# Weight splitting of the routed experts moved behind the last batch's gating in the shared-expert stage

## The reference

```
x2 = rmsnorm(hid, ln2_w)
logits = x2 @ gate_w.T
probs = softmax(logits);  top_w, top_i = top_k(probs, 4);  top_w /= top_w.sum()
routed = sum over the 4 chosen experts of top_w * (silu(g) * u) @ w2,   g, u = x2 @ w1
shared = (silu(sg) * su) @ sh_down_w.T,                                 sg, su = x2 @ sh_gu_w.T
out = hid + routed + shared
```

## Time and profile before

| | |
|---|---|
| median of 3 runs | 1240.77 us (1239.87 to 1243.07) |
| the profiled execution | 1242.91 us, with a span of 1241.2 us |
| PE busy, share of the span | 95% |
| DVE / ACT / POOL busy | 69% / 64% / 47% |
| mean granted clock of PE | 0.986 |
| shared-expert stage | 945.7 to 1012 us |
| tile loop | 1012 to 1199 us |

### The profile page before, as it was taken

One profiled execution on the slowest core, in us unless ns is written; L12 is line 12 of the kernel. 1 busy time (PEld: TensorE's weight loads), 2 busy tenths in 40 slices (PEclk: granted clock), 3 DMA queues, 4 the chain that ended last, 5 costly groups with the idle time before them and its releaser, 6 DMA issues.

```text
span 1241.2 us, 25176 instructions
## 1 busy us (share of the span) xinstructions
PE 1178.2 (95%) x7996; PEld 1007.7 (81%) x7996; DVE 861.5 (69%) x2662; ACT 794.0 (64%) x1971; POOL 577.1 (47%) x845
## 2 busy tenths in 40 slices
PE   6899999889999999999999999999998889999986
PEld 5756555579999998999989999989997769999962
DVE  5677887677667666886667876777865855555535
ACT  3387777767768776677676777776776534444422
POOL 3053645545333444537443366433363346666650
PEclk9989999999999999999999999999999989999998
DMA  8955555175733112122212122121214247777766
GB/s 266 283 160 174 172 167 152 51 213 152 213 109 95 54 55 87 48 70 83 86 35 69 35 68 105 35 68 35 69 61 113 68 124 122 117 118 119 117 113 218
DMA packets 111780, 139.59 MB, mean 112 GB/s; under 512 B 11364, under 2 KB 94820, under 8 KB 111524
## 3 DMA queue, kind: packets, MB, share of 16 engines
q1 hardware_dynamic: 97204, 119.10, 31.6%
q0 software_dynamic: 14448, 18.88, 9.4%
HBM read 63.36 MB, written 61.87 MB: 101 GB/s over the span
## 4 chain that ended last, share of the span: by engine, by line
PE 70%; DVE 12%; ACT 8%; issue 4%; POOL 3%; DMA 2%; SPq 1%; POOLq 0%; ACTq 0%; DVEq 0%
PE bank L1478 49%; PE bank L1887 5%; PE bank L1710 5%; DVE bank L1113 3%; PE bank L1527 3%; PE bank L1581 2%; ACT p L953 2%; PE bank L1564 2%; DVE hs L1336 2%; ACT pT L832 2%; DVE pT L1323 1%; PE bank L1866 1%; PE bank L1897 1%; PE bank L1571 1%; DVE qk L1212 1%
## 5 line engine op out<-in xcount | busy, mean ns | idle before, releaser
L1113 DVE CUSTOM_DVE_ANT_0 bank<-bank,mask 128x512 f32<-128x512 f32 (+3 forms) x512 | 235.2, 523 | 35.8 <-PE bank L1564 23.1
L944 ACT ACTIVATE p<-bank,stat 128x512 f32<-128x512 f32 (+3 forms) x256 | 131.7, 528 | 132.2 <-DVE stat L1113 132.2
L533 POOL CAST w_hl<-raw_qkv 128x512 fp32r<-128x512 f32 x96 | 58.8, 613 | 312.3 <-DMA raw_qkv<-in_qkvo 162.6
L1478 PE MATMUL bank<-xT,w_hl 128*128 128x512 f32 x768 | 189.2, 395 | 0.0
L1478 PEld LDWEIGHTS bank<-xT,w_hl 128*128 128x128 f32 x768 | 144.1, 188 | 34.1
L742 POOL DMA_INDIRECT sum_rows<-mid,goal x79 | 122.9, 1555 | 70.7 <-DVE mid L1442 69.2
L1478 PE MATMUL bank<-pT,v 128*128 128x128 f32 (+3 forms) x768 | 137.1, 327 | 0.0
L953 ACT ACTIVATE p<-p,stat 128x512 f32<-128x512 f32 (+3 forms) x256 | 123.1, 553 | 14.7 <-DVE stat L1339 14.7
L1478 PE MATMUL bank<-qk 128*128 128x512 f32 (+3 forms) x768 | 129.4, 317 | 3.2 <-DVE pT L1323 2.4
L1478 PEld LDWEIGHTS bank<-qk 128*128 128x128 f32 x768 | 119.3, 189 | 12.1 <-DVE v L1212 2.6
L534 POOL TENSOR_TENSOR w_hl<-raw_qkv,w_hl 128x512 fp32r<-128x512 f32 x96 | 124.2, 1294 | 7.8
(11 more groups left out here) (232 smaller groups left out, 2404.0 us busy)
## 6 DMA issues: line engine op xcount, KB each, us to landing
raw_qkv<-in_qkvo SPq DMA_DIRECT2D x32, 768.0 KB, 5.7
xs_rows<-blank SPq DMA_DIRECT2D x32, 520.0 KB, 3.3
xs_rows<-blank SPq DMA_DIRECT2D x5, 2730.0 KB, 14.3
xrow<-xs_rows SPq DMA_DIRECT2D x79, 130.0 KB, 2.5
raw_o<-in_qkvo SPq DMA_DIRECT2D x32, 256.0 KB, 3.7
sum_rows<-blank SPq DMA_DIRECT2D x3, 2176.0 KB, 8.5
stk<-xT SPq DMA_DIRECT2D x96, 64.0 KB
stk<-k_hl SPq DMA_DIRECT2D x96, 64.0 KB
```

What stands on the lines that cost most here:

```text
L944: act.activation(p2[:, n % 2, POFF[qi]:POFF[qi + 1]], s2(t), ACT.Exp, scale=-1.0, bias=stat2[:, 0, n % 2, t:t + 1], accum_out=stat2[:, 1, ...
L1113: return dve.tensor_tensor_reduce(scores, scores, mask[:, TB - scores.shape[1]:], scale=-1.0, scalar=-2.0 * MASKED, op0=ALU.add, op1=ALU.m ...
L1478: ins = pe.matmul(out, a, b, start=start and i == 0, stop=stop and i == len(pairs) - 1, **kw)
```

## The change

Four edits, none of which adds or removes an instruction.

1. ACT's four `w1_half` move from s = 0, 1, 6, 7 to s = 4, 6, 7, 8; DVE's four `w1_rest` from s = 1, 2, 10, 11 to s = 6, 7, 8, 10.
2. On DVE the sums of a finished batch (s = 3, 6, 9, 12) stand behind `hh_lo` and behind `probabilities` and `compare`, not ahead of them.
3. On PE the logits of the last batch stand ahead of `shared_down(1)`, not behind it.
4. PE's transpose of the tile table and DVE's copy into `tab` move from s = 7 to s = 8.

```
+        W1_STEPS, W1_REST_STEPS = (4, 6, 7, 8), (6, 7, 8, 10)
...
                 if s == 0:
-                    w1_half(0, 0)
                     norm_half(B - 1)
                 if s == 1:
                     for c in range(C):
                         take_x2(B - 1, c, bank[4 + c])
-                    w1_half(0, 1)
-                if s in (6, 7):
-                    w1_half(1, s - 6)
+                if s in W1_STEPS:
+                    w1_half(*divmod(W1_STEPS.index(s), 2))
                 if s in (5, 6, 7, 8):
                     fill_row(B - 1, s - 5)
...
                     dve.tensor_tensor(half, half, bank[2 + s % 2][0:rows, :], ALU.mult).then_inc(f_h, 1)
-                if s and s % SHR == 0:
-                    b = s // SHR - 1
-                    dve.wait_ge(f_dn, s)
-                    dve.wait_ge(r_row, TPB * (b + 1))
-                    for i in range(2):
-                        two = hs[:, TPB * b + 2 * i:TPB * b + 2 * i + 2, :].rearrange("p j d -> p (j d)")
-                        dve.tensor_tensor(two, two, bank[6 + i][:, :], ALU.add).then_inc(f_acc, 1)
                 if LO_POOL <= s < SHARED:
...
                 if s == 3:
                     probabilities(B - 1)
                     compare(range(0, 6))
+                if s and s % SHR == 0:
+                    b = s // SHR - 1
+                    dve.wait_ge(f_dn, s)
+                    dve.wait_ge(r_row, TPB * (b + 1))
+                    for i in range(2):
+                        two = hs[:, TPB * b + 2 * i:TPB * b + 2 * i + 2, :].rearrange("p j d -> p (j d)")
+                        dve.tensor_tensor(two, two, bank[6 + i][:, :], ALU.add).then_inc(f_acc, 1)
...
-                if s == 7:
+                if s == 8:
                     dve.wait_ge(r_tabT, 1)
                     dve.tensor_copy(tab[0:1, :], bank[4][0:1, 0:2 * P]).then_inc(r_tabi, 1)
-                if s >= SHARED - 2 and s < SHARED:
-                    w1_rest(1, s - SHARED + 2)
+                if s in W1_REST_STEPS:
+                    w1_rest(*divmod(W1_REST_STEPS.index(s), 2))
...
+                if s == 2:
+                    logits(B - 1, bank[4])
                 if s:
                     shared_down(s - 1)
...
-                if s == 2:
-                    logits(B - 1, bank[4])
...
-                if s == 7:
+                if s == 8:
                     pe.wait_ge(r_tab, 1)
```

More of the change, by code:

```diff
@@ L1401, in _ @@
                         take_x2(B - 1, c, bank[4 + c])
-                    w1_rest(0, 0)
                 if s == 2:
                     logits_less_max(B - 1, bank[4])
-                    w1_rest(0, 1)
                 if s == 3:
```

## The result

The changed kernel takes **1250.18 us** in the median of 5 runs (1248.46 to 1251.36), the kernel before 1243.07 in the median of its 5 runs (1239.87 to 1245.05): a ratio of 1.0059 with a 95% interval of 1.0043 to 1.0075, which is 5.3 to 9.3 us slower. The forecast was 1247.9, or +7.1; the difference of the medians is 7.1. The forecast counted from a median of three runs, 1240.77; with two more it is 1243.07, so the same step ends 2.3 us above the forecast time.

A forecast was written before the change was run, and what follows sets the result against it. The last send's landing was taken to set PE's loop start. Holds of 9.6 us, less the old hold 1.8 and the lead 0.7, gave +7.1 us: 1240.77 to 1247.9 us, forecast's own range 1244 to 1252.

The forecast's parts named there:

- What bounds it: Tile loop on PE: always busy, so a shift of its start, set by the last send's landing, shifts the end equally.
- The lead: Gating on DVE: wk written 0.7 us earlier, bounds 0.4 and 1.4, after POOL's hh_lo costs 0.7 to 1.0.
- The sends and `w_lo`: POOL's sends beside DVE: each of four w_lo holds one send until it ends, 9.6 us in all, 1.8 before.
- The phase: Sends against w_lo: a send beginning just before each w_lo makes every hold 1.8 and the sum +4.7 us.
- the prediction's last sentence: Sends beginning a little before each w_lo rather than after: every hold the small one, 1.8, sum +4.7 us.
- ACT's longer queue: ACT filling the third and fourth tiles, at 997.5 and 1002.5: hidden by the sends' own delay, ahead of their copies.
- The table's copy: DVE's copy into tab, a step later at 999.9: costs nothing, since SP waits for landings until 1016.
- PE's clock: PE at the loop's start: half-rate stretch (clock 0.66) taken as equal, with 1.5 us either way.
- the second rival: PE idles, then stays at half rate over steps 8 to 11: +12 to +14 us, 1253.5; chance 0.07.
- Rival 1: Sends not held by w_lo; third tile waits for ACT's xrow: +2.6 us, 1243.4, within 0.3%; chance 0.15.

The follow-up runs named there:

- e3: Changed kernel with the weight splitting back at its old steps (ACT 0, 1, 6, 7; DVE 1, 2, 10, 11), other three edits kept; 1242.89 us, ratio to before 1.0006.
- e5: Kernel before with the first edit alone (weight splitting at its new steps; sums, logits and table as before); 1247.40 us, ratio to before 1.0046.
- e1: Changed kernel with each w_lo's second operand from a PSUM bank, leaving out the subtraction of w_hi; 1241.49 us, ratio to before 0.9988.
- e11: Kernel before with the second operand of its last two w_lo from PSUM, leaving out that subtraction of w_hi; 1238.29 us, ratio to before 0.9976.
- e2: Changed kernel with each w_lo cut into four pieces, one behind the other; 1246.99 us, ratio to before 1.0035.
- e4: Changed kernel with ACT's fill_row ahead of w1_half in steps 6, 7 and 8; 1248.69 us, ratio to before 1.0053.
- e8: Changed kernel with each w_lo in four pieces and ACT's fill_row ahead of w1_half; 1247.28 us, ratio to before 1.0039.
- e9: Changed kernel with each w_lo in four pieces and the copy into tab behind the pieces of step 8; 1247.52 us, ratio to before 1.0045.

## Why the prediction was right, point by point

- **What bounds it.** Right: the loop's start carried over whole, 7.65 us there and 7.66 at the tail.
- **The lead** of 0.7 us in `wk` was 0.55. POOL's `hh_lo` beside the comparisons took its part: `compare`'s first instruction took 1.30 us in the changed kernel. But the lead hangs on the first edit alone: e3, without it, has `wk` 0.6 us late, and e5, with nothing else, has it 1.12 early. The working's parts came out: the probabilities at 967.25 (965.42 + 1.84), and the product of step 4 at 971.56, where 970.8 and the 0.7 to 1.0 of POOL's share give 971.5 to 971.8. What it did not ask is which edit gains. Against e5 the probabilities begin 1.8 us earlier (13.74, there 15.55), but the sums' 1.2 us follow before the product of step 4 all the same, and the earlier comparisons meet POOL's `hh_lo`: the other three edits together lose 0.57.
- **The sends and `w_lo`.** The step that carried the sum, from one send of 2.76 us. It is shown: with one operand in PSUM the hold is gone in both kernels (e1, e11), with shorter instructions it is shorter (e2), and it is in the first edit alone (e5). The four held sends and their order were as worked out; their holds were 9.6 by the working (2.0, 2.4, 2.5, 2.7) and 10.15 in the trace (1.84, 2.50, 2.91, 2.90). The whole was +7.1 by the working and +7.65 at the first tile. That the medians also differ by 7.1 to the tenth is luck, with an interval of 5.3 to 9.3. The phase was a near thing: two of the sends came 0.10 and 0.12 us behind the start of a `w_lo`. In e4 the fourteenth begins 0.38 us ahead of it, and the hold there is the small one, 1.79, as the prediction's last sentence has it. In e5 three of the four `w_lo` hold a copy, a case that the working left out.
- **ACT's longer queue** was hidden by the holds, as said: in e4 the first tile comes 0.45 us earlier and the ratio is 0.0006 lower, well inside both intervals. Its price without them is in e1: the last send begins 3.3 us later than in the kernel before, without holds.
- **The table's copy** a step later cost nothing: written at 998.6, while the last send landed at 1014.95.
- **PE's clock.** PE stood still for 1.84 us ahead of 984.70, 2.30 ahead of 993.00 and 1.81 ahead of 1005.18. The five-microsecond windows from 985 to 1015 have the clocks 0.66, 0.80, 0.86, 1.00, 0.66 and 1.00: half rate for a time after each, but not to the end of the stage; the second rival did not come. The prediction took the half-rate stretch at the loop's start as equal. It was (0.69 and 0.63 in the two five-microsecond windows from 1015, before 0.67 and 0.65 in the two from 1010), and e1 shows that it need not be.
- **Rival 1** is what e1 is: +2.6 us was said for no holds. At the first tile it was +3.2, at the tail +1.6, and in the median -1.0. Its mechanism held (the tile waits for `xrow`); its price left out that PE, hardly idle ahead of the loop, had clock 1.00 there. What makes the median lower still is not known.
## What to carry to other kernels

Where VectorE and GpSimd work side by side, list the VectorE instructions with two operands in SBUF and their lengths: here each held one GpSimd instruction that began inside it, an indirect DMA, a copy or a `tensor_tensor`, until it ended. Moving such an instruction off one chain is only a gain if GpSimd has nothing on the critical path where it lands; one send in a trace that is 2.9 times as long as its 63 fellows is reason enough to look at what VectorE did then. And look at what else moves when an order is changed for another reason: in e3 earlier logits put a VectorE instruction 0.1 us ahead of a GpSimd one, and the lead was gone; and sums that were moved back made TensorE wait for them.

## What the hardware showed that I had not expected

- An instruction of DVE that begins 0.1 us ahead of POOL's `hh_lo` made it 4.17 us in place of 1.29 (e3); in the other order, DVE's 0.08 us behind POOL's, it was DVE's addition that took 1.24 us. So the order of two starts 0.1 us apart decides which engine loses.
- A send that began inside the `hh_lo` of step 8 was held 3.6 to 4.1 us through four separate pieces of `w_lo` (e2, e8, e9), while sends that began inside a piece, or inside another `hh_lo`, were let go at its end. Open.
- With 1.1 us of idle time ahead of its last down product and hardly any ahead of the first tile, PE ran the loop's start at clock 1.00 (e1), where before, idle 1.15 us ahead of the one and 1.84 us ahead of the other, the clock was 0.66 over ten microseconds.
